# Four graph layers on 64 graphs: one whole exponential for the fourth graph of each group, written-out turns, the last bias on TensorE, and new instruction orders

## What is computed

```python
def att(x, adj):                     # x: [64,128,256], adj: [64,128,128]
    w = adj * exp((x @ Wq.T + bq) @ (x @ Wk.T + bk).T)
    return (w / w.sum(2)) @ (x @ Wv.T + bv)
def gcn(x, adj):                     # three layers, relu after the first two
    z = relu(adj @ (x @ W1) + b1); z = relu(adj @ (z @ W2) + b2)
    return adj @ (z @ W3) + b3
def hyper(x, adj):                   # incidence H = (adj != 0)
    conv = lambda x, W, b: Dn * (H @ (Be * (H.T @ (x @ W.T)))) + b
    return conv(layer_norm(relu(conv(x, W1, b1)), g, b), W2, b2) + x
def mha(x, adj):                     # 8 heads of 32
    s = softmax((q @ k.T) * 32 ** -0.5 * (adj + adj))
    return (s @ v).merge_heads() @ Wo.T + bo
for layer in (att, gcn, hyper, mha):
    x = layernorm(x + layer(x, adj))
```

## Time and profile before

| | us |
|---|---|
| median of 3 runs | 1083.41 |
| lowest, highest | 1082.42, 1085.48 |
| the profiled execution | 1082.07 |
| its span (first to last instruction) | 1080.1 |

### The profile page before, as it was taken

One profiled execution on the slowest core, in us unless ns is written; L12 is line 12 of the kernel. 1 busy time (PEld: TensorE's weight loads), 2 busy tenths in 40 slices (PEclk: granted clock), 3 DMA queues, 4 the chain that ended last, 5 costly groups with the idle time before them and its releaser, 6 DMA issues.

```text
span 1080.1 us, 23404 instructions
## 1 busy us (share of the span) xinstructions
PE 1032.4 (96%) x8404; PEld 914.6 (85%) x8404; DVE 800.7 (74%) x2186; ACT 679.1 (63%) x1980; POOL 481.4 (45%) x299
## 2 busy tenths in 40 slices
PE   8699999999999999999999999999999999998776
PEld 7588888888989888898988889898888889887665
DVE  4565868778696877869687787878687787778466
ACT  3345765949476593947669394856839485682814
POOL 2315253735345273534537363453636444351614
PEclk9999999999999999999999999999999999999998
DMA  5110200101011010101001010100101010100000
GB/s 224 49 60 1 68 3 30 60 30 58 10 50 37 19 58 29 58 20 58 19 19 58 29 58 29 58 10 19 58 29 58 29 58 10 31 1 20 2 30 20
DMA packets 17314, 42.42 MB, mean 39 GB/s; under 512 B 2048, under 2 KB 2048, under 8 KB 17152
## 3 DMA queue, kind: packets, MB, share of 16 engines
q1 hardware_dynamic: 17280, 41.97, 11.0%
HBM read 33.57 MB, written 8.39 MB: 39 GB/s over the span
## 4 chain that ended last, share of the span: by engine, by line
PE 69%; DVE 14%; ACT 7%; issue 6%; POOL 2%; DMA 0%; DVEq 0%; POOLq 0%; SPq 0%
PE ps L468 62%; PE ps L783 5%; ACT pr L940 5%; DVE mx L1242 3%; DVE pr L1237 3%; DVE x L1076 2%; DVE st L1060 2%; POOL rstd L1322 2%; PE ps L724 1%; DVE x L1122 1%; ACT fT_high L913 1%; DVE p L1113 1%; PE ps L654 1%; DVE mv L1069 1%; DMA pr<-in_weights 0%
## 5 line engine op out<-in xcount | busy, mean ns | idle before, releaser
L940 ACT ACTIVATE pr<-pr,mx 128x128 f32<-128x128 f32 x504 | 195.4, 396 | 12.4 <-DVE mx L1242 11.9
L1322 POOL TENSOR_TENSOR rstd<-var,neg_half 128x4 f32<-128x4 f32 (+1 forms) x84 | 73.4, 874 | 211.1 <-DVE var L1071 211.1
L1368 POOL TENSOR_TENSOR pr<-pr,den 128x1024 f32<-128x1024 f32 x64 | 121.1, 1901 | 72.5 <-DVE den L1257 72.5
L1076 DVE TENSOR_SCALAR x<-x,mv,rstd 128x256 f32<-128x256 f32 x256 | 88.7, 407 | 23.4 <-POOL rstd L1322 23.1
L1347 POOL TENSOR_TENSOR x<-x,rows 128x1024 f32<-128x1024 f32 x16 | 38.1, 2379 | 136.0 <-PE ps L468 136.0
L894 ACT COPY s_s<-ps 128x512 f32<-128x512 f32 x32 | 18.8, 587 | 126.0 <-PE ps L468 126.0
L940 ACT ACTIVATION_READ_ACCUMULATOR pr<-pr,mx 128x1 f32 x504 | 97.9, 194 | 0.0
L1060 DVE BATCH_NORM_STATS2 st<-x 128x6 f32<-128x256 f32 x256 | 93.8, 413 | 1.6
L1237 DVE TENSOR_TENSOR pr<-ps,adjB 128x1024 f32<-128x1024 f32 x64 | 75.3, 1217 | 24.1 <-PE ps L468 24.1
L1261 DVE COPY prT<-ps 128x512 f32<-128x512 f32 x64 | 42.8, 688 | 54.6 <-PE ps L783 54.5
L934 ACT ACTIVATE qkT<-ps,biases 128x512 f32<-128x512 f32 x64 | 42.2, 687 | 57.5 <-PE ps L468 55.6
(11 more groups left out here) (196 smaller groups left out, 3217.8 us busy)
## 6 DMA issues: line engine op xcount, KB each, us to landing
xT<-in_xT SPq DMA_DIRECT2D x16, 512.0 KB, 4.4
x<-in_x SPq DMA_DIRECT2D x16, 512.0 KB, 3.3
out_x<-x SPq DMA_DIRECT2D x32, 256.0 KB, 2.0
adjA<-in_adj SPq DMA_DIRECT2D x16, 256.0 KB, 4.7
adjTA<-in_adjT SPq DMA_DIRECT2D x16, 256.0 KB, 2.7
adjB<-in_adj SPq DMA_DIRECT2D x16, 256.0 KB, 4.5
pr<-in_weights SPq DMA_DIRECT2D x2, 512.0 KB, 6.4
qkT<-in_weights SPq DMA_DIRECT2D x1, 1024.0 KB, 12.4
```

The costliest lines, as they stand in the source:

```text
L940: act.activation(pr[:, b, k, :], pr[:, b, k, :], ACT.Exp, bias=mx[:, b, k:k + 1], accum_out=den[:, b, 0, k:k + 1]).then_inc(exp_ready, 1)
L1076: dve.tensor_scalar(t[:, b, :], t[:, b, :], mv[i][:, b, 0:1], rstd[i][:, b:b + 1], ALU.subtract, ALU.mult).then_inc(ready, 1)
L1322: pool.tensor_tensor(rstd[i][:, bs], var[i][:, bs], neg_half[:, bs], ALU.pow).then_inc(rstd_ready[i], len(pairs))
L1368: pool.tensor_tensor(pr[:, b], pr[:, b], den[:, b, 1, :].unsqueeze(2).broadcast_to([P, HEADS, P]), ALU.mult).then_inc(pr_ready, 1)
```

## The change

1. **Written-out turns.** The 12 middle turns are a Python loop over t, so their instructions stand in the program 12 times and no engine branches. The register arithmetic for semaphore values falls away.
2. **One exponential.** `WHOLE = (3,)` holds for every group: the fourth graph always goes by `mha_shift3`, one exponential and `mha_sum3`.
3. **The last group's bias of Wo** comes from PE: `mha_bias0` and `mha_bias1` each start a PSUM tile with a matmul of a row of ones by the bias row (512 columns), and the product with Wo is added to it. `x2_bias(1)` leaves POOL's list, and DVE's `mha_wo` of that group does not wait for it.
4. **Other tiles.** The last group's x1 is kept in tile x0 and its x2 in tile x.
5. **Three waits of PE fall away** (`v0_ready` in `att_out`, `adjTA_in` in `gcn_ax`, `v3_ready` in `mha_ctx`), all for things that an earlier wait of PE or of a step before it covers.
6. **New orders** in all three tables. The prologue has six `keep_busy` steps, where it had three; the epilogue four, where it had six, and none between `hyper_out` and the last group's `qk01`, where three stood.

The diff, cut. Of the tables the rows show only pieces; every engine's list is permuted.

```diff
-WHOLE = {1: (3,)}
+WHOLE = (3,)
...
-            with eng.Fori(3, NG - 1) as t:
+            for t in range(3, NG - 1):
...
+        def x1_of(g):
+            return x0 if final(g) else x1
+
+        def x2_of(g):
+            return x if final(g) else x2
...
             def att_out(g):
                 pe.wait_ge(p0T_ready, g + 1)
-                pe.wait_ge(v0_ready, GB * g + GB)
...
                     pe.wait_ge(x0_ready, GB * g + b + 1)
-                    if b == 0:
-                        pe.wait_ge(adjTA_in, 16 * g + 16)
...
-                pe.wait_ge(v3_ready, 2 * g + pair + 1)
...
+            def mha_bias(g, pair):
+                mm(ps2[:, 5 + 2 * pair], ones[0:1, :], r_o[0:1, :].unsqueeze(1).broadcast_to([1, 2, D]), 0, 2)
...
-                high_rows(ps2[:, 5 + 2 * pair, 0], "WoT", ctxT[:, :, 0, :], slice(0, P))
+                high_rows(ps2[:, 5 + 2 * pair, 0], "WoT", ctxT[:, :, 0, :], slice(0, P), C, final(g))
...
             def mha_exp_whole(g, b):
-                act.wait_ge(shift_ready, whole_before(g, b) + 1)
+                act.wait_ge(shift_ready, len(WHOLE) * g + WHOLE.index(b) + 1)
                 act.activation(pr[:, b], pr[:, b], ACT.Exp).then_inc(exp_ready, HEADS)
...
-                if whole(g, b):
-                    dve.wait_ge(sum_ready, whole_before(g, b) + 1)
+                if b in WHOLE:
+                    dve.wait_ge(sum_ready, len(WHOLE) * g + WHOLE.index(b) + 1)
...
-                dve.wait_ge(x2b_ready, g + 1)
+                if not final(g):
+                    dve.wait_ge(x2b_ready, g + 1)
```

More of the change, by code:

```diff
@@ L105 @@
-    "ACT": [("x_high", 0), ("high_Wv3T", 0), ("high_Wv0T", 0), ("high_WoT", 0), ("high_W2", 0), ("high_att", 0),
-        ("high_W1", 0), ("high_Wqk3T", 0), ("high_WupT", 0), ("att_t", 0), ("att_v0", 0), ("att_v1", 0),
-        ("att_off", 0), ("high_WdownT", 0), ("att_exp", 0), ("high_W3", 0), ("att_turn", 0), ("gcn_ax", 0),
-        ("x_split", 0), ("gcn_1", 0), ("gcn_2s0", 0), ("gcn_2s1", 0), ("gcn_2a", 0), ("gcn_3s0", 0), ("gram_turn", 0),
-        ("gcn_3s1", 0), ("att_v0", 1), ("att_t", 1), ("att_v1", 1), ("att_off", 1), ("att_exp", 1), ("att_turn", 1),
[10 rows of a table removed]
@@ L120 @@
-    "POOL": [("x_rest0", 0), ("att_t", 0), ("x0_stats0p", 0), ("x0_stats1p", 0), ("x_rest", 0), ("att_t", 1),
[5 rows of a table removed]
-    "SP": [("att_scores", 0), ("att_out", 0), ("att_turn", 0), ("gcn_3a1", 0), ("att_scores", 1), ("att_turn", 1),
-        ("att_out", 1), ("gcn_3a1", 1), ("att_scores", 2), ("mha_scores1", 0), ("att_out", 2), ("att_turn", 2),
+    "PE": [("keep_busy5", 0), ("set_att", 0), ("keep_busy4", 0), ("keep_busy0", 0), ("set_down", 0), ("att_t", 0),
+        ("att_t_rest", 0), ("att_v0", 0), ("att_v1", 0), ("att_scores", 0), ("set_wo", 0), ("att_turn", 0),
[4 rows of a table added]
+        ("att_scores", 1), ("hyper_x", 0), ("att_turn", 1), ("att_out", 1), ("hyper_up01", 0), ("gram", 1),
[13 rows of a table added]
@@ new lines @@
+    "DVE": [("set_rep", 0), ("set_att", 0), ("set_reps", 0), ("rest_att", 0), ("rest_Wv0T", 0), ("set_down", 0),
+        ("rest_Wqk3T", 0), ("rest_WoT", 0), ("incidence", 0), ("rest_Wv3T", 0), ("rest_W2", 0), ("rest_WupT", 0),
+        ("att_exp", 0), ("set_wo", 0), ("rest_WdownT", 0), ("rest_W1", 0), ("att_out", 0), ("att_res1", 0),
[20 rows of a table added]
+    "ACT": [("high_att", 0), ("high_W2", 0), ("high_Wv0T", 0), ("high_Wv3T", 0), ("high_WoT", 0), ("x_high", 0),
+        ("high_WupT", 0), ("high_Wqk3T", 0), ("high_WdownT", 0), ("att_v0", 0), ("att_t", 0), ("high_W1", 0),
+        ("att_v1", 0), ("att_off", 0), ("high_W3", 0), ("att_exp", 0), ("att_turn", 0), ("gcn_ax", 0), ("gcn_1", 0),
+        ("gcn_2s0", 0), ("gcn_2s1", 0), ("x_split", 0), ("gcn_2a", 0), ("gcn_3s0", 0), ("gcn_3s1", 0),
+        ("gram_turn", 0), ("att_t", 1), ("att_v0", 1), ("att_v1", 1), ("att_off", 1), ("att_exp", 1), ("att_turn", 1),
[16 rows of a table added]
@@ L128 @@
+    "SP": [("att_turn", 0), ("att_out", 0), ("att_scores", 0), ("gcn_3a1", 0), ("att_turn", 1), ("att_scores", 1),
+        ("att_out", 1), ("gcn_3a1", 1), ("att_turn", 2), ("att_scores", 2), ("mha_scores1", 0), ("att_out", 2),
         ("x3_norm0", 0), ("x3_norm1", 0)],
@@ L388, in turn_bank @@
             return 4 if b in (0, 3) else 6
-        def whole(g, b):
-            return isinstance(g, int) and NG - g in WHOLE and b in WHOLE[NG - g]
-        def whole_before(g, b):
-            return sum(len([k for k in graphs if NG - back < g or (NG - back == g and k < b)]) for back, graphs in WHOLE.items())
         def first(g):
@@ L476, in rest_pass, with high_rows, rest_rows @@
                 return mm(out, high[weight][:, c, cols], data_rest[:, c, :], 2 * C + c, 3 * C)
-            def high_rows(out, weight, data, n, chunks=C):
+            def high_rows(out, weight, data, n, chunks=C, begun=0):
                 for c in range(chunks):
-                    mm(out, data[:, c, n], high[weight][:, c, :], 2 * c, 3 * chunks)
-                    mm(out, data[:, c, n], rest[weight][:, c, :], 2 * c + 1, 3 * chunks)
-            def rest_rows(out, weight, data_rest, n, chunks=C):
+                    mm(out, data[:, c, n], high[weight][:, c, :], begun + 2 * c, begun + 3 * chunks)
+                    mm(out, data[:, c, n], rest[weight][:, c, :], begun + 2 * c + 1, begun + 3 * chunks)
+            def rest_rows(out, weight, data_rest, n, chunks=C, begun=0, more=0):
                 for c in range(chunks):
-                    last = mm(out, data_rest[:, c, n], high[weight][:, c, :], 2 * chunks + c, 3 * chunks)
+                    last = mm(out, data_rest[:, c, n], high[weight][:, c, :], begun + 2 * chunks + c, begun + 3 * chunks + more)
                 return last
@@ L663, in hyper_x @@
                     for c in range(C):
-                        last = mm(ps4[:, 6 + c, b], x1[:, b, c * P:(c + 1) * P], gmT[:, b, :])
+                        last = mm(ps4[:, 6 + c, b], x1_of(g)[:, b, c * P:(c + 1) * P], gmT[:, b, :])
                 last.then_inc(gx_done, 1)
@@ L723, in mha_xt @@
                     for c in range(C):
-                        last = pe.transpose(ps4[:, 6 + c, b], x2[:, b, c * P:(c + 1) * P], ident[:])
+                        last = pe.transpose(ps4[:, 6 + c, b], x2_of(g)[:, b, c * P:(c + 1) * P], ident[:])
                 last.then_inc(x2T_done, 1)
@@ L973, in _ @@
             run(act, "ACT", {
-                "x_high": x_high, **{f"mha_exp{b}": lambda g, b=b: mha_exp_whole(g, b) for b in range(GB)},
+                "x_high": x_high, **{f"mha_exp{b}": lambda g, b=b: mha_exp_whole(g, b) for b in WHOLE},
                 **{f"high_{name}": set_high(name) for name in PARTED},
@@ L1226, in hyper_out @@
                 bs = slice(2 * k, 2 * k + 2)
-                dve.scalar_tensor_tensor(out=x2[:, bs, :], in0=x1[:, bs, :], scalar=2.0, in1=ps2[:, 4 + k], op0=ALU.mult,
+                dve.scalar_tensor_tensor(out=x2_of(g)[:, bs, :], in0=x1_of(g)[:, bs, :], scalar=2.0, in1=ps2[:, 4 + k], op0=ALU.mult,
                                          op1=ALU.add).then_inc(res2_ready, 1)
@@ L1266, in mha_wo @@
                     dve.wait_ge(out_stored, 32 * g)
[L1267 removed]
+                if not final(g):
+                    dve.wait_ge(x2b_ready, g + 1)
                 bs = slice(2 * pair, 2 * pair + 2)
[L1269 removed]
+                dve.tensor_tensor(x3[:, bs, :], ps2[:, 5 + 2 * pair], x2_of(g)[:, bs, :], ALU.add).then_inc(res3_ready, 1)
             run(dve, "DVE", {
[L1272 to L1273 removed]
+                **{f"mha_shift{b}": lambda g, b=b: mha_shift(g, b) for b in WHOLE},
+                **{f"mha_sum{b}": lambda g, b=b: mha_sum(g, b) for b in WHOLE},
                 "set_rep": set_rep, "set_reps": set_reps, "set_att": set_att, "set_down": set_down, "set_wo": set_wo,
```

32 lines of the change are left out of this document (12 added, 20 removed), and 299 rows, old and new, of tables (EPILOGUE, PROLOGUE, SCHEDULE).

## The result

| us | before | changed |
|---|---|---|
| median (runs) | 1082.91 (4) | 1071.05 (4) |
| lowest, highest | 1080.4, 1085.48 | 1069.87, 1071.08 |
| profiled execution | 1082.07 | 1069.87 |
| its span | 1080.1 | 1068.1 |

Against the kernel before as it was measured beside the experiments (medians of 1081.4 to 1082.1) it is 10.4 to 11.0 us. The profiled execution is the fastest of the changed kernel's four: its mean granted clock was 0.993, that of the other three 0.988 to 0.989.

The account below looks back on a forecast made before the run. PE, busy 96% of the span, was taken as the bound, with waits worth much only at the ends. Turns -0.6, prologue -2.8 and last two turns -0.5 gave -3.9: from 1083.41 to 1079.5 us, range 1072 to 1088.

Parts of the forecast that it names:

- The turns: Twelve middle turns: each 62.45 us instead of 62.50, -0.6 us in all, bounds -7.6 and +8.3.
- Written-out turns at 0: Middle turns: branch hidden behind queued work, register arithmetic free on DVE and ACT; 0, bounds 4.2 us either way.
- The list of waits: PE in a middle turn: only two waits, 0.38 us at hyper_x and 0.25 at gcn_ax; the rest matmuls.
- The place of p and the norm: DVE's new order in a turn: hyper_x wins 0.2 us, norm of x0 at 448.25 against 448.21, gm just fits.
- both waits go: Rival, middle turns: masks early enough and p too; -7.6 us in the turns, total 1072.5, chance 0.18.
- The prologue: Ahead of the middle turns: splits, whole exponential and fills sum to -2.8 us, between -5 and +1.
- The splits: Prologue on DVE: WdownT's split moves behind p, -1.2 us; two 512-column splits leave the chain, -1.2 for both.
- The extra fills: Prologue on PE: three more keep_busy steps, 2.8 us of matmuls, mostly covered by waits; +0.5, at most +2.8.
- The last two turns: End of the kernel: earlier div1, whole exponential, pow on POOL and lower clock sum to -0.5 us, between -4 and +3.
- The turn gets longer: Rival, middle turns: late p, norm and gm delay PE at att_turn, gcn_ax, gcn_1; +8.3 us, total 1088.4, chance 0.20.
- The ends give nothing: Rival, prologue and last turns: PE meets the next wait where the first is removed; total 1082.8, chance 0.12.
- the code is not free: Rival, written-out middle turns: one wait of 0.35 us a turn, +4.2 us, total 1083.7, chance 0.08.

Follow-up runs that it names:

- k1: The kernel before with only its twelve middle turns written out: 1077.93 us, ratio 0.997, a turn 62.34 us.
- k10: The changed kernel with the middle order of before, the shift behind the scaling to gm: 1072.80 us, a turn 62.08 us.
- k2: The changed kernel with its middle turns as a hardware loop again: 1071.84 us, a turn 62.09 us.
- k7: The changed kernel with the epilogue's orders of before and the last group's bias on POOL again: 1069.64 us.
- k12: The changed kernel with three keep_busy steps put back into the last turn: 1068.98 us, ratio 0.9875 to the kernel before.
- k5: The changed kernel with the middle order of before, the shift ahead of the scaling to gm: 1078.64 us, a turn 62.60 us.

## Why the prediction was wrong, point by point

**The turns (-0.6 forecast, -6.8 measured in eleven periods, so -7.4 in twelve).** Of the 0.62 us a turn, 0.16 is the written-out code, 0.26 the whole exponential, 0.20 the new order on top of it, in the sequence before, k1, k10, changed.

- *Written-out turns at 0.* The step that failed is the comparison of the earlier trace rows. It shows that the branch is hidden at the turn's edge, and that was right. It says nothing of the register arithmetic inside the turn, which came to 0.1 us where an engine that PE waits for, or PE itself, stood at a wait: on DVE ahead of the first masks, on PE ahead of `gcn_ax`. I wrote that it takes no time of its own on DVE and ACT, and did not ask for PE.
- *The list of waits.* I named two waits of PE in a turn and called the rest matmuls end to end. There was a third: the second gcn matrix waited for the rest of z1. In the kernel before, one of its matmuls started 0.29 us behind the last where 0.12 is usual, and the next 0.33 where 0.24 is usual, at 459.81 and 460.14. The page's marks do not show it, only the distances of the starts do. I had costed ACT's 2.1 us only by whether PE waits for the context's copy, and not followed what is queued behind that copy on ACT. This is the largest part: 0.26 us a turn in k10.
- *The place of p and the norm.* The walk's results were near: `hyper_x` 0.56 us behind the transposes (I had some 0.5), gm 0.34 us ahead of need (I had 0.06), the shift at 1.22 us. The wait for `gcn_ax`, which I left where it was, went: in the changed kernel it starts 0.47 us behind the two matmuls of 512 columns ahead of it, their own time. Up to `gcn_1` the new order wins 0.13 of its 0.20 us over k10; the rest comes in smaller pieces behind. The `dn` operations cost 0.47 us there and DVE won 0.5 back, because with the residuals and the four statistics in one piece the stretch to the variance fell from 6.02 to 5.57 us (5.68 with the loop, k2). I had allowed 0.3 for it.

The case *both waits go* had nearly the size, -7.6 in the turns, but that is luck: of its two waits 0.21 us is left ahead of `hyper_x`, and more than half of the gain came from the third wait and the loop, which it does not name.

**The prologue (-2.8 forecast, -4.4 measured).** The term up to the first gcn matrix was right: I put it near 41, and it stands here in the changed kernel, against 43.30:

```profile
41.07 0.47 PE L470 MATMUL ps<-fT_high,W_high 128*128 128x512 f32 x1 [0.77 <-ACT fT_high L874]
```

The splits did move off the chain as told. The extra fills cost nothing that shows: the second p transposes are 2.7 us earlier, so the gain grew where I had set +0.5. A term at nothing was the clock: it fell once in this stretch before (0.92 from 28 to 50 us) and not now (1.00). By k1, where it was 0.84 and the way from the first to the second transposes 0.8 us longer, I estimate that this fall cost some 0.8 us. The whole exponential, for which I had 0.9, gave 1.4 in the period to group 3. The sum was mis-sized by 1.6 us because I followed one chain, priced the fills only as work, and took the rest of 180 us as unchanged.

**The last two turns (-0.5 forecast, -0.8 measured).** That the sum is near is luck: k1, with the orders of before, took 203.54 us for the stretch where the kernel before took 205.02, so 0.8 is less than one execution differs from another, and the parts were off. `div1` starts earlier, but for the one wait of 2.87 us PE now has two, of 0.93 and 1.45. The clock is lower, as I said: 0.84 from the x2 transposes to the first scores, where it was 1.00, and 10.47 us against 9.08 with the old epilogue (k7), +1.4 where I had +1.0. But the missing fills are not shown to be the cause, since k12 has them and the same 0.84. The bias on POOL I called free; in the new epilogue it costs some 2 us. I had taken for the picture of POOL and held that the fourth multiply waits for the exponential anyway, while the whole exponential and its sum leave only 0.64 us of slack there. And I took the shift at 1.22 us only with POOL idle: in the last but one turn, where POOL is not, it took 2.91 us (last section), though the chain of the page runs over ACT there.

**The rivals.** *The turn gets longer* did not happen in the changed kernel, but k5 shows that its mechanism is real, at 0.52 us a turn over k10 where I priced 0.69: the shift ahead of gm stops PE if DVE arrives as late as before. *The ends give nothing* and *the code is not free* are refuted by the table and by k1. The shares were wrong on the fast side: the low bound should have held both waits gone and the prologue's own bound of -5, 1083.4 - 7.6 - 5 - 0.5 = 1070.3.

## What to carry to other kernels

Where one engine is busy all the time, list its waits by the distances of its starts, not by the marks, and for each follow what is queued behind the late step on the other engine: here a context copy on ACT that PE did not wait for delayed a relu that it did wait for. An engine's freed time is worth something only where a queue ends in such a wait; freeing 2.1 us on ACT won 0.26 to 0.47 us a turn. To price a loop, look between a wait and the instruction behind it on every engine, not at the loop's edge. And an instruction added on an engine with time to spare should be tried on both sides of the step that another engine waits for: shift ahead of gm or behind it is 62.60 or 62.08 us a turn.
